# A four-layer transformer kernel on one core: turned tiles among the dense products, weight casts in ScalarE's gaps, and a score bank for attention's last group

## The chip, the cores and the metric

The kernel runs on one core of one Trainium2 chip. The metric is the device time of one execution in microseconds, lower is better. A core has TensorE (PE, which loads weights through PEld), VectorE (DVE), ScalarE (ACT), GpSimd (POOL) and SyncE (SP, which here issues the DMAs). TensorE writes into eight PSUM banks of 2 KB a partition; the other engines read the results from there.

## The reference

Four layers work on 1,024 tokens of 256 features. Each layer is `x = x + s * silu(f)`, where `s` is a token mixer and `f` a feed-forward part, both computed from the same layer-normalised `xn`. The change touches the way from the third layer to the fourth, and the fourth layer's attention.

```
xn = layernorm(x)                       # third layer
s = attention over 16 heads @ w_dense
f = 8 gated experts, weighted per token
x = x + s * silu(f)
xn = layernorm(x)                       # fourth layer
q, k, v = xn @ wq.T, xn @ wk.T, xn @ wv.T      # 8 heads, q and k in two halves each
y = softmax(rms(q1) rms(k1)) v - lambda * softmax(rms(q2) rms(k2)) v   # causal
s = y @ wo.T * 0.2
f = fwht(silu(xn @ W1.T) * (xn @ W3.T)) @ W2.T
out = x + s * silu(f)
```

## The kernel before

Every engine has its own instruction list, written out by hand; the engines meet only at semaphores (`wait_ge`). The tokens stand in 8 tiles of 128 (t = 0 to 7) and in 4 quarters of two tiles (i = 0 to 3). For precision each product of two float32 matrices is made of three products of rounded parts: `product` (L102 to L104) multiplies rounded by rounded, rounded by rest and rest by rounded. The rounded part of an operand comes from a cast, mostly on ScalarE, and its rest from a subtraction on VectorE or GpSimd.

From the third layer to the fourth the work goes like this.

- TensorE makes the last expert's down products (banks 4 to 7) and the dense products of attention (banks 0 to 3) in two halves, tiles 0 to 3 and then tiles 4 to 7.
- VectorE adds the expert's result into `g_tok` (`add_expert`, L1943); ScalarE puts it through Silu (`gate_silu`, L2322); VectorE multiplies by the dense product and adds to x (`residual`, L1456 and L1457), takes mean and variance (`statistics`, L1462 to L1468); GpSimd raises to the power of -1/2 (`rsqrt`, L657); VectorE normalises (`normalised`, L1473).
- TensorE transposes the normalised tiles (`turn_xn`, L888) into bank i for quarter i, ScalarE casts the quarter from there (`turned`, L2131) and VectorE takes its rest (`turned_rest`, L1480). Only then can TensorE make q, k and v of the tiles in that quarter (`qkv_rows`), which ScalarE evicts (`qkv_copy`, L2380 and L2383).
- TensorE's order is: all dense products, turned tiles 0 to 3, q/k/v of tiles 0 to 2, turned tiles 4 to 7, q/k/v of tiles 3 to 7. Its q/k/v products rotate over the bank pairs 6-7, 4-5 and 0-1.
- VectorE's order is: residuals and normalised tiles of the first half, `add_expert` of tiles 4 to 7, the rests of quarters 0 and 1, and then the same for the second half.
- ScalarE also casts the fourth layer's gate weights in four parts (L2474), and GpSimd subtracts to get their rests (L853), two parts at a time. These rests stand ahead of the gate and up products (`w_gate3`, `w_up3`), which follow the q/k/v products on TensorE. GpSimd takes the four `rsqrt(3)` before the gate rests, and the squares for the rms (L859) after them.

Attention of the fourth layer runs over 24 units (`UNITS3`): a unit is a pair of key tiles for a half of the queries of one group of four heads. `scores3` (L1373) writes a unit's scores for two heads at a time into one of three pairs of banks, 0-1, 2-3 and 4-5, in turn; ScalarE takes the exponential (L2511); for the units on the diagonal GpSimd multiplies by the causal mask, two instructions of two heads each (L875); `values3` (L1387), two units later, multiplies by v and by ones. The units of one (group, half) add up in one bank: the 16 results (`MIXES3`) alternate between banks 6 and 7, and VectorE divides (`normalise`, a reciprocal at L2079 and a product at L2081). So the last result, made of units 22 and 23, waits until the result two before it is divided. Behind the attention TensorE makes the down products, each waiting for a rest that VectorE takes (L2093), and the output products.

Of the kernel before, what the change touches and what calls it, by code (L numbers as in the profile page):

```python
# [45 lines left out]
E2 = 8  # L46
# [73 lines left out]
def build(nc, a, out, layers=4):  # L120
    ctx = ExitStack()
    with ctx:
# [210 lines left out]
        LAG3 = 2  # L333
        HID3_AT, HID3_BEHIND = (9, 12), (6, 8)
# [128 lines left out]

        SPLIT = [True, True, True, True]

        QKV_BANK = [None, None, (0, 6), (6, 4, 0)]
        QKV_TURNED = [None, None, (0, 0), (0, 0, 1)]
# [176 lines left out]
        def _(pool):  # L644
# [195 lines left out]
            if layers > 3:  # L840
# [30 lines left out]
                for u in DIAGONAL3:  # L871
                    for i in range(2):
# [7 lines left out]
        def _(pe):  # L880
# [301 lines left out]
            def qkv_rows(w, w_hi, layer, tiles=range(NT)):  # L1182

                turns = len(QKV_BANK[layer])
                for t in tiles:
                    if t >= turns:
                        pe.wait_ge(qkv_done, 2 * (NT * (layer - 2) + t - turns) + 2)
                    b0 = QKV_BANK[layer][t % turns]
                    turned(layer, QKV_TURNED[layer][t] if t < turns else t // 2)
# [74 lines left out]
            if layers > 2:  # L1264
# [44 lines left out]
                for b in range(B):  # L1309
# [5 lines left out]
                    for t in tiles:  # L1315
# [4 lines left out]
                        mm.then_inc(s_ready, 1)  # L1320
            if layers > 3:

                turn_xn(3, range(ST))
                pe.wait_ge(wq_split, 2)
                pe.wait_ge(e2_done, E20 + 8 * E2)
                qkv_rows(w_qkv3, w_qkv3_hi, 3, range(3))
                turn_xn(3, range(ST, NT))
                qkv_rows(w_qkv3, w_qkv3_hi, 3, range(3, NT))
# [50 lines left out]
                def mix3(m, u, which):  # L1379
# [3 lines left out]
                    for kt, at, q0, w in blocks_of(u):  # L1383
                        for hh in range(4):
                            head = 4 * c + hh
                            lhs = ones[:, 0:32] if which else v3[:, ST * b + kt, 32 * head:32 * head + 32]
                            mm = pe.matmul(bank[6 + m % 2][32 * hh:32 * hh + 32, 256 * which + q0 - 256 * h:256 * which + 256],  # L1387
# [5 lines left out]
                def values3(u):  # L1393
                    g, h, k = UNITS3[u]
                    m = MIXES3.index((g, h))
                    if u in DIAGONAL3:
                        pe.wait_ge(causal_done, 2 * DIAGONAL3.index(u) + 2)
                    else:
                        pe.wait_ge(exp3_done, 2 * u + 2)
                    if u == GROUPS3[m][0] and m >= 2:  # L1400
# [34 lines left out]
        def _(dve):  # L1435
# [469 lines left out]
            if layers > 2:  # L1905
# [101 lines left out]
                if layers > 3:  # L2007
                    add_expert(E2 - 1, 1, last=True, tiles=range(ST, NT))
                    rests(3, 0)
                    residuals(2, 1)  # L2010
                    rests(3, 1)
            if layers > 3:
# [59 lines left out]
                def normalise(m):  # L2072
                    g, h = MIXES3[m]
                    b, c, j = g // 4, g // 2 % 2, g % 2
                    o = bank[6 + m % 2]
# [18 lines left out]

                for m in range(len(MIXES3)):
                    normalise(m)
# [27 lines left out]
        def _(act):  # L2124
# [248 lines left out]
            def qkv_copy(layer, first=0, end=NT, between=None):  # L2373
                for t in range(first, end):
                    act.wait_ge(qkv_ready, NT * (layer - 2) + t + 1)
                    b0 = QKV_BANK[layer][t % len(QKV_BANK[layer])]
# [88 lines left out]
            if layers > 3:  # L2465

                turned(3, (0, 1))
                gate_silu(2, (2, 3))
                qkv_copy(3, 0, 2)
                turned(3, (2, 3))  # L2470
                qkv_copy(3, 2, 3)
                act.wait_ge(wgo3_in, 32)
# [122 lines left out]
```

## Time and profile before

| what | value |
|---|---|
| time, median of 3 runs | 840.95 us (840.45 to 841.15) |
| the profiled execution's own time | 839.71 us |
| its span in the trace | 837.9 us |
| TensorE busy | 826.0 us, 99% of the span |
| VectorE busy | 624.9 us, 75% |
| ScalarE busy | 478.4 us, 57% |
| GpSimd busy | 471.2 us, 56% |
| granted TensorE clock | 1.00 over the span |

The span runs from the first to the last instruction of the trace; the execution's own time has 1.81 us more around it. A busy share says how long an engine had an instruction in it. A matmul's end is modelled, and matmuls overlap, so the distance between the starts of two matmuls tells what one costs, and its own duration does not.

### The profile page before, as it was taken

The page shows a single profiled execution, that of the slowest core. Times are in us where ns is not written, and L with a number is a line of the kernel's source. Part 1 is how long each engine was busy: PE and PEld are TensorE (multiplying, and loading weights), DVE is VectorE, ACT ScalarE, POOL GpSimd, SP SyncE. Part 2 cuts the span into 40 slices and gives each one's busy share as a digit, 9 for nine tenths or more (in the row PEclk, how much of TensorE's full clock was granted, in tenths as well). Part 3 has the DMA queues.
Part 4 walks back from the last instruction along what each step waited for, and adds up shares of the span by engine and source line. Part 5 has one row for each costly group of instructions (what it writes and reads, how often), then busy time and mean ns, then how long its engine had stood idle before and what let it go on. Part 6 is the DMA issues. An engine that isn't in the chain of part 4 may idle for free.

```text
span 837.9 us, 15615 instructions
## 1 busy us (share of the span) xinstructions
PE 826.0 (99%) x5436; PEld 709.6 (85%) x5436; DVE 624.9 (75%) x1267; ACT 478.4 (57%) x953; POOL 471.2 (56%) x327
## 2 busy tenths in 40 slices
PE   8999999999999999999999999999999999999998
PEld 7888888888867899999999888888889988876688
DVE  6899999999997665665567788687676785436767
ACT  3666666666674565655553475743453435367743
POOL 6676767677684855575757021019948316718820
PEclk9999999999999999999999999999999999999999
DMA  8101010000005385556313150011111010030001
GB/s 340 43 20 38 19 38 19 28 28 19 19 1 188 146 283 184 184 166 193 110 32 94 59 201 14 1 52 51 38 38 38 14 63 1 1 151 4 2 2 51
DMA packets 23345, 62.19 MB, mean 74 GB/s; under 512 B 3137, under 2 KB 13633, under 8 KB 20225
## 3 DMA queue, kind: packets, MB, share of 16 engines
q1 hardware_dynamic: 21760, 57.35, 19.8%
q0 software_dynamic: 1536, 4.20, 1.6%
q8 instruction: 30, 0.49, 0.2%
q14 instruction: 19, 0.15, 0.1%
HBM read 50.00 MB, written 8.39 MB: 70 GB/s over the span
## 4 chain that ended last, share of the span: by engine, by line
PE 88%; DVE 6%; POOL 2%; ACT 2%; issue 1%; DMA 1%; SPq 0%; DVEq 0%; POOLq 0%
PE banks L102 26%; PE banks L104 26%; PE banks L103 26%; PE banks L1387 3%; POOL arenaC L875 1%; PE banks L1373 1%; PE banks L1023 1%; PE banks L967 1%; PE banks L966 1%; DVE x L1457 1%; DVE arenaB L1892 1%; PE banks L888 1%; PE banks L1010 1%; PE banks L1056 1%; DMA arenaC<-in_wqkv 1%
## 5 line engine op out<-in xcount | busy, mean ns | idle before, releaser
L2153 ACT ACTIVATE banks<-banks,small 128x512 f32<-128x512 f32 x128 | 84.9, 664 | 70.8 <-DVE small L1522 70.8
L1522 DVE TENSOR_REDUCE small<-banks 128x1 f32<-128x512 f32 x128 | 86.7, 677 | 4.4 <-PE banks L104 4.4
L104 PE MATMUL banks<-arenaC_rounded,arenaD_rounded 128*128 128x512 f32 (+1 forms) x256 | 89.4, 349 | 0.0
L102 PE MATMUL banks<-xnT_rounded,arenaD_rounded 128*128 128x512 f32 x224 | 87.8, 392 | 1.1 <-POOL arenaC_rounded L741 0.9
L103 PE MATMUL banks<-s_tok_rounded,arenaD_rounded 128*128 128x512 f32 x224 | 87.2, 389 | 0.0
L104 PE MATMUL banks<-xnT_rounded,arenaD_rounded 128*128 128x512 f32 x192 | 74.8, 390 | 0.0
L104 PE MATMUL banks<-xnT_rounded,arenaC_rounded 128*128 128x512 f32 x192 | 74.7, 389 | 0.0
L102 PE MATMUL banks<-arenaC_rounded 128*128 128x512 f32 (+1 forms) x192 | 70.9, 369 | 1.2 <-DVE arenaC L1537 0.6
L1537 DVE SCALAR_TENSOR_TENSOR arenaC<-banks,small,arenaC 128x512 f32<-128x512 f32 x96 | 71.2, 741 | 0.0
L103 PE MATMUL banks<-arenaD_rounded,arenaC_rounded 128*128 128x512 f32 (+1 forms) x192 | 67.9, 354 | 0.0
L727 POOL TENSOR_TENSOR arenaD_rounded<-arenaC,ones 128x512 fp32r<-128x512 f32 x30 | 31.3, 1042 | 47.4 <-DVE arenaC L1537 46.5
L102 PE MATMUL banks<-arenaB_rounded,arenaC_rounded 128*128 128x256 f32 (+2 forms) x172 | 55.4, 322 | 0.0
L104 PEld LDWEIGHTS banks<-arenaC_rounded,arenaD_rounded 128*128 128x128 f32 x256 | 48.0, 188 | 5.0
L657 POOL TENSOR_TENSOR rstd<-veps,mhalf 128x2 f32<-128x2 f32 x16 | 12.2, 762 | 69.1 <-DVE veps L1468 69.1
L788 POOL TENSOR_TENSOR arenaD_rounded<-arenaD,arenaB_rounded 128x1024 fp32r<-128x1024 f32 (+1 forms) x12 | 37.6, 3147 | 23.7 <-ACT arenaB_rounded L2217 23.7
L102 PEld LDWEIGHTS banks<-xnT_rounded,arenaD_rounded 128*128 128x128 f32 x224 | 42.0, 188 | 10.0 <-POOL arenaC_rounded L741 1.0
L102 PE MATMUL banks<-xnT_rounded,arenaB_rounded 128*128 128x512 f32 x128 | 50.3, 393 | 0.0
L103 PEld LDWEIGHTS banks<-s_tok_rounded,arenaD_rounded 128*128 128x128 f32 x224 | 42.1, 188 | 8.5
L103 PE MATMUL banks<-arenaC_rounded,arenaB_rounded 128*128 128x320 f32 (+2 forms) x144 | 49.1, 341 | 0.0
L722 POOL TENSOR_TENSOR arenaD_rounded<-arenaD,arenaC_rounded 128x512 fp32r<-128x512 f32 x32 | 41.5, 1297 | 12.6 <-ACT arenaD L2144 12.6
L104 PE MATMUL banks<-arenaB_rounded,arenaC_rounded 128*128 128x256 f32 (+1 forms) x140 | 46.1, 329 | 0.0
L103 PE MATMUL banks<-arenaB_rounded,arenaC_rounded 128*128 128x320 f32 (+2 forms) x140 | 45.8, 327 | 0.0
(445 smaller groups left out, 2689.3 us busy)
## 6 DMA issues: line engine op xcount, KB each, us to landing
arenaD<-in_wexp SPq DMA_DIRECT2D x8, 1060.0 KB, 5.8
arenaD<-in_wexp SPq DMA_DIRECT2D x8, 1024.0 KB
arenaC<-in_wqkv SPq DMA_DIRECT2D x16, 384.0 KB, 3.0
arenaD<-in_wexp SPq DMA_DIRECT2D x8, 512.0 KB, 3.6
slots<-arenaB SPq DMA_DIRECT2D x1, 2560.0 KB, 9.9
arenaB<-in_sw SPq DMA_DIRECT2D x1, 2084.0 KB, 7.5
arenaC<-in_wo SPq DMA_DIRECT2D x1, 2048.0 KB, 15.3
arenaC<-slots SPq DMA_DIRECT2D x8, 256.0 KB, 3.2
```

Of the source, the lines that this page charges most:

```text
L102: pe.matmul(o, r(lhs[0]), r(rhs[0]), start=start, stop=False)
L103: pe.matmul(o, r(lhs[0]), r(rhs[1]), start=False, stop=False)
L104: return pe.matmul(o, r(lhs[1]), r(rhs[0]), start=False, stop=stop)
L657: pool.tensor_tensor(rstd[:, sl], veps[:, sl], mhalf[:, sl], ALU.pow).then_inc(ln_rstd, 1)
L722: pool.tensor_tensor(r(klo[q][:, sl]), klo[q][:, sl], rounded(kT[q][:, sl]), ALU.subtract).then_inc(klo_done, 1)
L727: pool.tensor_tensor(r(acc_hi[b]), acc[b], ones[:, 0:1].to_broadcast([P, S]), ALU.mult).then_inc(acc_rounded, 1)
L788: pool.tensor_tensor(r(v), v, rounded(h), ALU.subtract).then_inc(w_split, 1)
L875: pool.tensor_tensor(d, d, con[:, C_CAUSAL:C_CAUSAL + P].unsqueeze(1).unsqueeze(1).to_broadcast([P, 2, 2, P]), ALU.mult).then_inc(causal_d ...
L1387: mm = pe.matmul(bank[6 + m % 2][32 * hh:32 * hh + 32, 256 * which + q0 - 256 * h:256 * which + 256], lhs, prob3[u % 4][:, hh, at:at + w], ...
L1522: dve.tensor_reduce(negmax[:, n % 4:n % 4 + 1], bank[3 + n % 4][:, :], AX.X, ALU.max, negate=True).then_inc(max_done, 1)
L1537: ins = dve.scalar_tensor_tensor(acc[n // ST], prob[n % 4], inv, acc[n // ST], ALU.mult, ALU.add)
L2153: act.activation(prob[r], prob[r], ACT.Exp, bias=negmax[:, r:r + 1], accum_out=rowsum[:, r:r + 1]).then_inc(exp_done, 1)
```

## The change

It has two parts. Between the layers, TensorE turns tiles 0 and 1 ahead of the last dense product, tiles 2 and 3 behind it, tiles 4 and 5 behind the q/k/v products of tile 2, and tiles 6 and 7 behind those of tile 4. The q/k/v products use an explicit list of banks (`QKV_BANK`) and of the tile whose eviction they wait for (`QKV_BEFORE`). VectorE takes the rest of quarter 0 right behind the first half's normalised tiles, and does the second half quarter by quarter. ScalarE mixes the weight casts, the Silu of the fourth quarter and the evictions in another order. In attention, the last result goes to bank 4 and its wait for an earlier division is left out, and the second two heads of unit 22 are masked by VectorE (`masked_last`, ahead of the division of result 13) in place of GpSimd.

```
@@ -331,6 +331,10 @@
         DIAGONAL3 = [n for n, (g, h, k) in enumerate(UNITS3) if k == 2 * h]
         GROUPS3 = [[u for u, v in enumerate(UNITS3) if v[0:2] == mix] for mix in MIXES3]
         LAG3 = 2
+
+        def mix_bank(m):
+            return 6 + m % 2 if m < len(MIXES3) - 1 else 4
+
         HID3_AT, HID3_BEHIND = (9, 12), (6, 8)
         TURNS3 = {6: (0, 1), 8: (2, 3), 10: (4, 5), 12: (6, 7)}
 
@@ -461,10 +465,12 @@
 
         EXP0, ACC0, VALS0, HID0, Y0, TURN0, ROWS0, GU0, E20 = 4, 4, 1, 0, 2, 2, 32, 2, 8
 
+        causal_dve = gold_done
         SPLIT = [True, True, True, True]
 
-        QKV_BANK = [None, None, (0, 6), (6, 4, 0)]
-        QKV_TURNED = [None, None, (0, 0), (0, 0, 1)]
+        QKV_BANK = [None, None, (0, 6) * 4, (4, 0, 4, 0, 6, 0, 4, 6)]
+        QKV_BEFORE = [None, None, (None, None, 0, 1, 2, 3, 4, 5), (None, None, 0, 1, None, 3, 2, 4)]
+        QKV_TURNED = [None, None, (0, 0), (0, 1)]
         HAD_BANK, LIN_BANK = (0, 1, 4, 5), (0, 1, 4, 5)
         TURNED_BANK = [(0, 1, 2, 3), (2, 3, 6, 7), (4, 5, 2, 3), (0, 1, 2, 3)]
         S0_BANK = (0, 5)
@@ -869,7 +875,7 @@
                 pool.tensor_tensor(r(v), v, rounded(hi), ALU.subtract).then_inc(had_done, 1)
 
                 for u in DIAGONAL3:
-                    for i in range(2):
+                    for i in range(2 if u != DIAGONAL3[-1] else 1):
                         pool.wait_ge(exp3_done, 2 * u + i + 1)
                         d = prob3[u % 4].rearrange("p h (k n) -> p h k n", k=2)[:, 2 * i:2 * i + 2, :, 0:P]
                         pool.tensor_tensor(d, d, con[:, C_CAUSAL:C_CAUSAL + P].unsqueeze(1).unsqueeze(1).to_broadcast([P, 2, 2, P]), ALU.mult
@@ -1181,12 +1187,11 @@
 
             def qkv_rows(w, w_hi, layer, tiles=range(NT)):
 
-                turns = len(QKV_BANK[layer])
                 for t in tiles:
-                    if t >= turns:
-                        pe.wait_ge(qkv_done, 2 * (NT * (layer - 2) + t - turns) + 2)
-                    b0 = QKV_BANK[layer][t % turns]
-                    turned(layer, QKV_TURNED[layer][t] if t < turns else t // 2)
+                    if QKV_BEFORE[layer][t] is not None:
+                        pe.wait_ge(qkv_done, 2 * (NT * (layer - 2) + QKV_BEFORE[layer][t]) + 2)
+                    b0 = QKV_BANK[layer][t]
+                    turned(layer, QKV_TURNED[layer][t] if t < 2 else t // 2)
                     n1 = D + E2 if layer == 2 else D
                     for o, w0, n in ((bank[b0][:, :], 0, 512), (bank[b0 + 1][:, 0:n1], 512, n1)):
                         for c in range(DC):
@@ -1318,14 +1323,20 @@
                                          [ctxT[:, c, t * P:(t + 1) * P], ctx_tok[:, t, c * P:(c + 1) * P]],
                                          [w_dense_hi[:, c, :], w_dense[:, c, :]], c == 0, c == DC - 1)
                         mm.then_inc(s_ready, 1)
+                        if layers > 3 and t == NT - 2:
+                            turn_xn(3, (0, 1))
             if layers > 3:
 
-                turn_xn(3, range(ST))
+                turn_xn(3, (2, 3))
                 pe.wait_ge(wq_split, 2)
+                pe.wait_ge(e2_done, E20 + 8 * (E2 - 1) + ST)
+                qkv_rows(w_qkv3, w_qkv3_hi, 3, range(3))
+                turn_xn(3, (4, 5))
+                qkv_rows(w_qkv3, w_qkv3_hi, 3, (3,))
                 pe.wait_ge(e2_done, E20 + 8 * E2)
-                qkv_rows(w_qkv3, w_qkv3_hi, 3, range(3))
-                turn_xn(3, range(ST, NT))
-                qkv_rows(w_qkv3, w_qkv3_hi, 3, range(3, NT))
+                qkv_rows(w_qkv3, w_qkv3_hi, 3, (4,))
+                turn_xn(3, (6, 7))
+                qkv_rows(w_qkv3, w_qkv3_hi, 3, (5, 6, 7))
                 pe.wait_ge(qkv_done, 4 * NT - 4)
 
                 def turn_qk(t):
@@ -1384,7 +1395,7 @@
                         for hh in range(4):
                             head = 4 * c + hh
                             lhs = ones[:, 0:32] if which else v3[:, ST * b + kt, 32 * head:32 * head + 32]
-                            mm = pe.matmul(bank[6 + m % 2][32 * hh:32 * hh + 32, 256 * which + q0 - 256 * h:256 * which + 256],
+                            mm = pe.matmul(bank[mix_bank(m)][32 * hh:32 * hh + 32, 256 * which + q0 - 256 * h:256 * which + 256],
                                            lhs, prob3[u % 4][:, hh, at:at + w],
                                            start=(u == GROUPS3[m][0] and at == 0 and which == 0), stop=(u == GROUPS3[m][-1] and at > 0 and which == 1),
                                            tile_position=(0, 32 * hh))
@@ -1393,11 +1404,14 @@
                 def values3(u):
                     g, h, k = UNITS3[u]
                     m = MIXES3.index((g, h))
-                    if u in DIAGONAL3:
+                    if u == DIAGONAL3[-1]:
+                        pe.wait_ge(causal_done, 2 * len(DIAGONAL3) - 1)
+                        pe.wait_ge(causal_dve, 2)
+                    elif u in DIAGONAL3:
                         pe.wait_ge(causal_done, 2 * DIAGONAL3.index(u) + 2)
                     else:
                         pe.wait_ge(exp3_done, 2 * u + 2)
-                    if u == GROUPS3[m][0] and m >= 2:
+                    if u == GROUPS3[m][0] and 2 <= m < len(MIXES3) - 1:
                         pe.wait_ge(norm3_done, m - 1)
                     mix3(m, u, 0)
                     mm = mix3(m, u, 1)
@@ -2005,10 +2019,18 @@
                 add_expert(E2 - 1, 1, last=True, tiles=range(ST))
                 residuals(2, 0)
                 if layers > 3:
-                    add_expert(E2 - 1, 1, last=True, tiles=range(ST, NT))
-                    rests(3, 0)
-                    residuals(2, 1)
-                    rests(3, 1)
+                    turned_rest(3, 0)
+                    add_expert(E2 - 1, 1, last=True, tiles=(4, 5))
+                    turned_rest(3, 1)
+                    residual(2, 2)
+                    statistics(3, 2)
+                    add_expert(E2 - 1, 1, last=True, tiles=(6, 7))
+                    normalised(3, 2)
+                    residual(2, 3)
+                    turned_rest(3, 2)
+                    statistics(3, 3)
+                    normalised(3, 3)
+                    turned_rest(3, 3)
             if layers > 3:
 
 
@@ -2072,7 +2094,7 @@
                 def normalise(m):
                     g, h = MIXES3[m]
                     b, c, j = g // 4, g // 2 % 2, g % 2
-                    o = bank[6 + m % 2]
+                    o = bank[mix_bank(m)]
                     dve.wait_ge(av_ready, m + 1)
                     if m:
                         dve.wait_ge(norm3_done, m)
@@ -2092,7 +2114,17 @@
                     v = hid3[:, :, t * P:(t + 1) * P]
                     dve.tensor_tensor(r(v), v, rounded(hid3_hi[t % 2]), ALU.subtract).then_inc(gu_split, 1)
 
+                def masked_last():
+
+                    u = DIAGONAL3[-1]
+                    dve.wait_ge(exp3_done, 2 * u + 2)
+                    d = prob3[u % 4].rearrange("p h (k n) -> p h k n", k=2)[:, 2:4, :, 0:P]
+                    dve.tensor_tensor(d, d, con[:, C_CAUSAL:C_CAUSAL + P].unsqueeze(1).unsqueeze(1).to_broadcast([P, 2, 2, P]), ALU.mult
+                                      ).then_inc(causal_dve, 1)
+
                 for m in range(len(MIXES3)):
+                    if m == len(MIXES3) - 3:
+                        masked_last()
                     normalise(m)
                     if m in HID3_BEHIND:
                         hid3_rest(HID3_BEHIND.index(m))
@@ -2373,7 +2405,7 @@
             def qkv_copy(layer, first=0, end=NT, between=None):
                 for t in range(first, end):
                     act.wait_ge(qkv_ready, NT * (layer - 2) + t + 1)
-                    b0 = QKV_BANK[layer][t % len(QKV_BANK[layer])]
+                    b0 = QKV_BANK[layer][t]
                     qk, v = (qkv2[:, t, 0:512], qkv2[:, t, 512:768]) if layer == 2 else (qk3[:, t, :], v3[:, t, :])
                     if layer == 2:
                         act.copy(z_raw[:, t, :], bank[b0 + 1][:, D:D + E2]).then_inc(z_copied, 1)
@@ -2465,16 +2497,23 @@
             if layers > 3:
 
                 turned(3, (0, 1))
-                gate_silu(2, (2, 3))
+                gate_silu(2, (2,))
                 qkv_copy(3, 0, 2)
-                turned(3, (2, 3))
+                gate_silu(2, (3,))
+                act.wait_ge(wgo3_in, 32)
+
+                def up_gate_round(parts):
+                    for n in parts:
+                        act.copy(r(part(arenaB, 1536 + 512 * n, 512)), part(arenaD, 3072 + 512 * n, 512)).then_inc(ff3_rounded, 1)
+
+                up_gate_round((0,))
+                turned(3, (2,))
                 qkv_copy(3, 2, 3)
-                act.wait_ge(wgo3_in, 32)
-                for n in range(4):
-                    act.copy(r(part(arenaB, 1536 + 512 * n, 512)), part(arenaD, 3072 + 512 * n, 512)).then_inc(ff3_rounded, 1)
-                    if n % 2:
-                        qkv_copy(3, 3 + n // 2, 4 + n // 2)
-                qkv_copy(3, 5)
+                up_gate_round((1,))
+                qkv_copy(3, 3, 4)
+                up_gate_round((2, 3))
+                turned(3, (3,))
+                qkv_copy(3, 4)
 
                 def queries3(t):
                     act.wait_ge(qkT_ready, t + 1)
```

## Rows read from the trace of the kernel before

**Rows 1.** The page, busy time of an engine, its share and its instructions.

```profile
PE 826.0 (99%) x5436; PEld 709.6 (85%) x5436; DVE 624.9 (75%) x1267; ACT 478.4 (57%) x953; POOL 471.2 (56%) x327
```

**Rows 2.** The timeline of TensorE between the layers: start, duration, instruction, count, idle before.

```profile
679.42 0.28 PE L102 MATMUL banks<-arenaB_rounded 128*128 128x256 f32 x1
...
680.12 1.04 PE L888 MATMUL banks<-con,xn 128*128 128x128 f32 x8
682.55 0.47 PE L102 MATMUL banks<-arenaB_rounded,xnT_rounded 128*128 128x512 f32 x1 [1.39 <-DVE arenaC_rounded L1480]
...
688.92 1.40 PE L888 MATMUL banks<-con,xn 128*128 128x128 f32 x8
690.07 0.48 PE L102 MATMUL banks<-arenaB_rounded,xnT_rounded 128*128 128x512 f32 x1
...
700.65 0.39 PE L102 MATMUL banks<-xnT_rounded,arenaB_rounded 128*128 128x512 f32 x1
```

**Rows 3.** The timeline of TensorE at sixteen earlier transposes.

```profile
666.97 1.91 PE L1306 MATMUL banks<-con,arenaB 128*128 128x128 f32 x16
668.63 0.36 PE L102 MATMUL banks<-xn_rounded,arenaD_rounded 128*128 128x256 f32 x1
```

**Rows 4.** The timeline of VectorE in the same stretch.

```profile
679.49 0.74 DVE L1473 TENSOR_SCALAR xn<-x,meanvar,rstd 128x256 f32<-128x256 f32 x2 [0.26 <-POOL rstd L657]
680.14 1.66 DVE L1943 SCALAR_TENSOR_TENSOR g_tok<-banks,small,g_tok 128x256 f32<-128x256 f32 x4
681.71 0.69 DVE L1480 TENSOR_TENSOR arenaC_rounded<-banks,xnT_rounded 128x512 fp32r<-128x512 f32 x1
...
685.50 0.69 DVE L1456 TENSOR_TENSOR g_tok<-g_tok,banks 128x512 f32<-128x512 f32 x1
...
688.02 0.17 DVE L1468 TENSOR_SCALAR veps<-meanvar 128x2 f32<-128x2 f32 x1
...
689.09 0.41 DVE L1473 TENSOR_SCALAR xn<-x,meanvar,rstd 128x256 f32<-128x256 f32 x1 [0.26 <-POOL rstd L657]
```

**Rows 5.** The timeline of ScalarE in the same stretch.

```profile
680.76 1.07 ACT L2131 CAST xnT_rounded<-banks 128x512 fp32r<-128x512 f32 x2 [7.42 <-PE banks L888]
681.72 1.16 ACT L2322 ACTIVATE g_tok<-g_tok 128x512 f32<-128x512 f32 x2
...
685.40 0.38 ACT L2383 COPY arenaC<-banks 128x256 f32<-128x256 f32 x1
```

**Rows 6.** The timeline of GpSimd in the same stretch.

```profile
692.82 4.78 POOL L853 TENSOR_TENSOR arenaD_rounded<-arenaD,arenaB_rounded 128x1024 fp32r<-128x1024 f32 x2 [3.76 <-ACT arenaB_rounded L2474]
```

**Rows 7.** The timeline of TensorE at attention's end.

```profile
800.57 0.83 PE L1387 MATMUL banks<-arenaC,ones 128*32 128x256 f32 x16
801.72 0.86 PE L1387 MATMUL banks<-arenaB,arenaC 128*32 128x256 f32 x16 [0.32 <-DVE arenaC L2081]
802.36 0.43 PE L1387 MATMUL banks<-arenaB,ones 128*32 128x256 f32 x4
```

**Rows 8.** The timelines of ScalarE and GpSimd at attention's end.

```profile
797.54 1.51 ACT L2511 ACTIVATE arenaB<-banks 128x768 f32<-128x768 f32 x2 [0.53 <-PE banks L1373]
...
798.87 2.54 POOL L875 TENSOR_TENSOR arenaB<-arenaB,con 128x512 f32<-128x512 f32 x2
```

**Rows 9.** The timeline of VectorE at attention's end and behind it.

```profile
799.36 1.76 DVE L2079 RECIPROCAL arenaC<-banks 128x256 f32<-128x256 f32 x1 [2.11 <-PE banks L1387]
...
809.14 1.23 DVE L2093 TENSOR_TENSOR arenaB_rounded<-arenaB,arenaD_rounded 128x1024 fp32r<-128x1024 f32 x1 [1.91 <-ACT arenaD_rounded L2500]
```

**Rows 10.** Lines L1918, L1473 and L2026 of VectorE, the second with shortest, median and longest ns.

```profile
663.37 1.80 DVE L1918 TENSOR_TENSOR arenaD_rounded<-arenaD,xn_rounded 128x512 fp32r<-128x512 f32 x1
...
L1473 DVE TENSOR_SCALAR xn<-x,meanvar,rstd x32: 404/408/420, 6.0 to 689.4; 128x256 f32<-128x256 f32 x32
...
710.03 0.29 DVE L2026 TENSOR_SCALAR small<-small 128x256 f32<-128x256 f32 x1
```

**Rows 11.** The timeline of GpSimd ahead of L1918's long case.

```profile
663.33 1.30 POOL L846 TENSOR_TENSOR arenaC_rounded<-arenaC,arenaB_rounded 128x512 fp32r<-128x512 f32 x1 [16.20 <-ACT arenaB_rounded L2457]
```

## The prediction

> **What bounds the kernel now.** I read the page first: TensorE is busy for 826.0 us of a span of 837.9 [rows 1], at the full granted clock all along. So only about 12 us can be won without taking matmuls away, and an edit that takes none away is worth exactly the TensorE waits that it ends. I then listed TensorE's gaps over the stretch that the change touches, from 667 us to the end, in its timeline.
>
> Between the layers there are two. The dense products end at 680.12, eight transposes follow, and the first q/k/v product starts at 682.55, released by VectorE's rest of quarter 0 [rows 2]. Sixteen transposes elsewhere take 668.63 - 666.97 = 1.66, so 0.104 each [rows 3]; eight need 0.83, and the first gap holds 2.43 - 0.83 = 1.60 of waiting. The second group of eight takes 690.07 - 688.92 = 1.15 [rows 2], so 0.32 is waiting: tiles 6 and 7 are normalised only from 689.09 on [rows 4]. Together 1.92.
>
> At attention's end the first products of unit 22 start at 801.72, behind a division on VectorE [rows 7]. The products before them started at 800.57. The same sixteen take 802.36 - 801.72 = 0.64 right after [rows 7], so unit 22 could have started at 800.57 + 0.65 = 801.22. That gap is worth 0.50; the trace calls 0.32 of it idle, since it counts from a modelled end.
>
> All that the change can give is therefore 1.92 + 0.50 = 2.42.
>
> **Between the layers, step by step.** No matmul, cast or subtraction is added or taken away; two groups of transposes become four, and SyncE's DMAs stay where they are. I follow the new order with the old durations.
>
> 1. Tiles 0 and 1 are turned at 679.42, where the last dense product started [rows 2]. They must be normalised by then: the pair 2 and 3 starts on VectorE at 679.49 [rows 4], so they are. Before, ScalarE's cast began 680.76 - 680.12 = 0.64 behind the first transpose [rows 2, 5], with four needed for it. Now it begins at 680.06 and, at half of 1.07 [rows 5], ends at 680.6.
> 2. VectorE is at its normalised tiles until 679.49 + 0.74 = 680.23 [rows 4], and then takes the rest at once, where before it first added the expert into four tiles (1.66) [rows 4]. The rest starts at about 680.68. Before, the first product stood 682.55 - 681.71 = 0.84 behind the rest's start [rows 2, 4]. So TensorE starts at 681.52, 1.03 earlier. Its own work by then ends at 679.42 + 8 x 0.104 + 0.70 (the dense tile) = 680.95: 0.57 of the wait stays, since the chain transpose, cast, rest is as long as it was.
> 3. Three tiles of q/k/v take 688.92 - 682.55 = 6.37, so 2.12 each [rows 2]. Tile 1 now needs quarter 1's rest, at 683.64. VectorE adds the expert into tiles 4 and 5 (0.83) and takes that rest until about 682.8. It is in time by 0.8.
> 4. Quarter 2: the residual starts at 682.8; residual and statistics take 688.02 - 685.50 = 2.52 up to the variance, and the normalised tiles start 689.09 - 688.02 = 1.07 later [rows 4], which is 686.4. They end at 687.15, and TensorE wants them at 681.52 + 6.37 = 687.89. In time. It turns them, makes tile 3 until 687.89 + 0.42 + 2.12 = 690.43, and needs quarter 2's rest there; the chain of step 2 gives it by 690.0.
> 5. Quarter 3 is the tight one. Its Silu stands on ScalarE behind the eviction of tile 1. Before, tile 0 left TensorE at 682.55 + 2.12 = 684.67 and its eviction ended at 685.40 + 0.38 = 685.78 [rows 2, 5], 1.1 later. Tile 1 now leaves at 685.76, so the Silu (0.58, half of 1.16 [rows 5]) ends at 687.45. The residual ends at 687.45 + 2 x 0.70 = 688.85, then quarter 2's rest comes in between until 689.8, statistics take 2.52 - 1.4 = 1.1, and the tiles start at 691.95. Tile 6 is normalised by 692.3 and tile 7 by 692.7. TensorE comes at 690.43 + 2.12 = 692.55 and turns tile 6 until 692.76. So it waits 0 to 0.2, where before it waited 0.32.
> 6. Tiles 5 to 7 follow: 692.55 + 0.42 + 6.37 = 699.34, to which I add 0.1 for step 5. Before, the gate products started at 700.65 [rows 2]. The gain is 1.2; two more changes between transposes and products, which no row prices apart, can take 0.1 to 0.2 of it.
>
> What must not become late is the gate rests on GpSimd, 4.78 for both [rows 6]. They need ScalarE's casts, of which the first pair is ready at about 690.7 (behind tile 2's eviction, 1.1 from 689.1 on, and 0.54 for a part of 512 columns, as half of 1.07 [rows 5]), and they stand behind the last `rsqrt`, which now ends at about 691.9 (before, it had ended ahead of 689.09). They run from 691.9 to 696.7 instead of 692.82 to 697.60, and the products want them at 699.4. They are covered by 2.7; without that cover each microsecond of lateness would cost one. The squares behind them gain only 0.9, where TensorE gains 1.2.
>
> **Attention's end.** The bank: without the division, unit 22 waits for its mask only. GpSimd's two masks run from 798.87 to 801.41 [rows 8], so the bank alone would give 801.72 - 801.45, about 0.3. The mask: GpSimd ends the first half at 798.87 + 1.27 = 800.14. VectorE can start the other at 797.54 + 1.51 = 799.05, when both exponentials are done [rows 8]; it is free, since its next division waits until 799.36 [rows 9]. The price on VectorE has no row of this kind. From below it is the 0.69 of a subtraction of the same 512 columns [rows 4]. From above it is 1.80: the row of L1918 with two SBUF inputs, started 0.04 behind a GpSimd instruction of 1.30 [rows 10, 11]. It looks like 1.26 of waiting and 0.6 of work. GpSimd's mask started first here too, so I take the end at 800.14 + 0.69 = 800.83. Even 799.05 + 1.80 = 800.85 is ahead of 801.22, so the whole 0.50 is won. Divisions 13 and 14 start up to 1.5 late; behind the last one VectorE had 1.91 idle ahead of L2093 [rows 9].
>
> The Trainium skill says the same of that pair (SBUF — State Buffer, section "SBUF: two separate sides"): GpSimd and a VectorE instruction with two SBUF inputs, or in a two-port mode, take one shared port pair as an exclusive lock for the whole instruction. By this rule, the trace agrees with L1918's 1.80 against 0.69.
>
> **The sum.** 1.2 + 0.5 = 1.7. The profiled execution would have a span of 836.2 and, with the same 1.81 around it, 838.0 instead of 839.71. The median of the runs is 1.24 above the profiled one, so the forecast is 840.95 - 1.7 = 839.25, which I round up to 839.3 for the two switches.
>
> **The rivals.** 0.2% of 840.95 is 1.68 us, about what a measurement of this kernel can tell from no change; the forecast stands at that bound.
>
> - Step 5 slips (17 in 100). Quarter 3's chain crosses three engines, with ScalarE's eviction in it; 0.5 to 1.0 more lateness at tile 6 goes straight to TensorE. Gain 0.7 to 1.2, time 839.7 to 840.2. For it: the margin is zero. Against: all durations are read from rows.
> - Only attention's end works, or the gain between the layers comes back as a wait among the gate products, because the squares and the root behind them gained less (8 in 100). Gain 0 to 0.6, time 840.4 to 841. Against it: the squares lose only 0.3 relative to TensorE.
> - More than forecast (7 in 100): the 0.57 of step 2 shrinks too, up to the full 2.42. Time 838.5.
> - Slower, by the port (8 in 100, half of it beyond 0.2%). GpSimd's first gate rest (2.39, half of 4.78 [rows 6]) now starts at 691.9, together with VectorE's last two normalised tiles; before, it started behind them. If L1473 has to wait as L1918 did, tile 6 comes at 691.9 + 2.39 + 0.35 = 694.6 and TensorE stalls by some 2.3: 841.6, no change to be told. If the second rest gets in ahead of tile 7 as well, it is 4.7: 840.95 - 1.7 + 4.7 = 843.95. It decides from a stall of 3.4 on. Against it: L1473 has one SBUF tensor as its input. The rival needs it to hold both ports all the same, and no row has it beside a long GpSimd instruction.
>
> A page speaks for this last rival. The Trainium skill (VectorE: DVE Perf Modes, section "The perf-mode tier table") lets a float32 `tensor_scalar` in SBUF run at twice the speed, with both read ports. By it L1473 would be locked out, and the result would be the 841.6 to 843.95 above. The trace speaks against it here: L1473, with its scalars read from SBUF, takes 408 ns for 256 columns, and L2026, with constants, 293 ns for the same 256 [rows 10]. Only L2026 looks like the faster mode.
>
> **How the numbers follow.** The forecast's case (60 in 100) spans 838.9 to 839.7, so gains of 1.25 to 2.05, with somewhat more of it below the bound of 839.27 than above in speed: 35 of the 60 are faster by over 0.2%. With the 7 for more, faster has 42 in 100; slower 5; no change to be told 53. The range of 838.5 to 841.0 takes in all but the slower rival and what lies outside of the sum.
>
> **What would show it.** The first q/k/v product starts 1.0 behind the last dense one (681.52 - 680.54, with 0.42 of transposes in it), not 2.43; VectorE's rest of quarter 0 directly behind its normalised tiles; no idle time at the second and fourth groups of transposes; GpSimd's gate rests about 0.9 earlier and the gate products 1.2 earlier; L1473 at 0.41 beside GpSimd; and unit 22 starting without a wait, with VectorE's mask ending ahead of it. The prediction is wrong if TensorE waits for tile 6, for a gate rest, or among the gate products, or if VectorE's mask takes over 2.1.

## The result, and the profile after

The changed kernel takes 845.67 us in the median (5 runs, 844.09 to 846.07), the kernel before beside it 841.04. The ratio is 1.0051, with a 95% interval of 1.004 to 1.0061: it is slower by 4.6 us, and the forecast was 1.7 us faster. The profiled execution took 845.67 with a span of 843.9, 6.0 above the span before.

I cut both spans at the same four events: the start of the last group that belongs to the dense products (the last dense tile before, tiles 0 and 1 turned after), the first gate product, the first score and the first down product.

| stretch | before | after | difference |
|---|---|---|---|
| up to the dense products' last tile | 679.42 | 680.85 | +1.43 |
| to the first gate product | 21.23 | 26.21 | +4.98 |
| to the first score | 47.26 | 47.35 | +0.09 |
| to the first down product | 56.97 | 56.43 | -0.54 |
| to the end | 33.02 | 33.06 | +0.04 |

The first 1.43 lies ahead of everything that the change touches. In the executions profiled below that point lies between 678.9 and 681.1, at both ends in kernels with the changed order, so it is no effect of the change. The stage with attention's end (the last but one) gave 0.54, where 0.5 was forecast. All of the loss is between the layers. These are TensorE's rows there, which answer to [rows 2]; the columns are start, duration, instruction, count and the idle time before it.

```profile
680.85 0.60 PE L894 MATMUL banks<-con,xn 128*128 128x128 f32 x4
...
682.95 0.47 PE L102 MATMUL banks<-arenaB_rounded,xnT_rounded 128*128 128x512 f32 x1 [0.35 <-DVE arenaC_rounded L1494]
...
689.29 0.60 PE L894 MATMUL banks<-con,xn 128*128 128x128 f32 x4
...
695.85 0.41 PE L894 MATMUL banks<-con,xn 128*128 128x128 f32 x2 [1.76 <-DVE xn L1487]
698.10 0.69 PE L894 MATMUL banks<-con,xn 128*128 128x128 f32 x2 [1.85 <-DVE xn L1487]
698.44 0.78 PE L102 MATMUL banks<-arenaB_rounded,xnT_rounded 128*128 128x512 f32 x1
...
707.06 0.39 PE L102 MATMUL banks<-xnT_rounded,arenaB_rounded 128*128 128x512 f32 x1
```

The first half went as planned: the first q/k/v product stands 2.10 behind the start of the last dense group, where it stood 3.13 before. Tiles 4 and 5 are turned without a wait. Then TensorE waits 1.76 for tile 6 and 1.85 for tile 7, and VectorE's line L1487 (L1473 before) is what it waits for. VectorE's and GpSimd's timelines, and the line's shortest, median and longest time, show why.

```profile
692.54 0.69 POOL L663 TENSOR_TENSOR rstd<-veps,mhalf 128x2 f32<-128x2 f32 x1 [4.80 <-DVE veps L1482]
693.19 4.71 POOL L859 TENSOR_TENSOR arenaD_rounded<-arenaD,arenaB_rounded 128x1024 fp32r<-128x1024 f32 x2
...
693.27 4.78 DVE L1487 TENSOR_SCALAR xn<-x,meanvar,rstd 128x256 f32<-128x256 f32 x2 [0.81 <-POOL rstd L663]
...
L1487 DVE TENSOR_SCALAR xn<-x,meanvar,rstd x32: 404/408/2434, 6.0 to 695.6; 128x256 f32<-128x256 f32 x32
```

GpSimd starts its first gate rest at 693.19, VectorE its tile 6 at 693.27. Two instructions that took 0.74 [rows 4] now take 4.78, next to the 4.71 of GpSimd's two, and end 0.15 behind them (698.05 and 697.90). A second loss is in the products behind. The windows give the busy time of each engine, then the granted clock of TensorE (PEclk).

```profile
core 0: us, PE busy (x) PEld busy (x) DVE busy (x) ACT busy (x) POOL busy (x), PEclk, DMA share, GB/s
692.50:698.44 5.94, 2.33 (x14) 1.76 (x13) 4.78 (x2) 1.42 (x4) 5.90 (x4) 0.84 0.00 0
698.44:703.30 4.86, 4.86 (x17) 4.09 (x16) 3.13 (x8) 1.98 (x5) 3.29 (x4) 0.50 0.02 3
703.30:708.00 4.70, 4.70 (x28) 4.08 (x27) 2.75 (x4) 1.84 (x5) 3.29 (x4) 0.99 0.00 0
```

Behind the two waits TensorE runs 4.86 us at 0.50, its lower level of 1.2 GHz, and loses half of that, 2.43 by this estimate. The clock fell here during the second wait: it was 1.00 up to 696 and 0.50 from 697 on. Attention's end, which answers to [rows 7 to 9], is clean: unit 22 follows unit 21 after 0.65 and without a wait, and VectorE's mask ends at 807.20.

```profile
805.37 1.29 POOL L881 TENSOR_TENSOR arenaB<-arenaB,con 128x512 f32<-128x512 f32 x1
...
805.57 1.63 DVE L2122 TENSOR_TENSOR arenaB<-arenaB,con 128x512 f32<-128x512 f32 x1 [1.83 <-ACT arenaB L2550]
...
807.05 0.83 PE L1398 MATMUL banks<-arenaC,ones 128*32 128x256 f32 x16
807.70 0.83 PE L1398 MATMUL banks<-arenaB,arenaC 128*32 128x256 f32 x16
```

### The profile page after: what moved, and what is told of

It reads as the page before. It is cut to its first block, busy times and chain, and to the rows that moved or that the text cites. A ratio compares the mean times of both kernels' runs of the same rounds, so it can differ in the third digit from the quotient of the medians.

```text
span 843.9 us, 15619 instructions
## 1 busy us (share of the span) xinstructions
PE 829.9 (98%) x5436; PEld 712.7 (84%) x5436; DVE 630.7 (75%) x1268; ACT 478.7 (57%) x953; POOL 470.0 (56%) x326
## 4 chain that ended last, share of the span: by engine, by line
PE 88%; DVE 6%; POOL 2%; ACT 2%; DMA 1%; issue 1%; SPq 0%; DVEq 0%; POOLq 0%
PE banks L102 26%; PE banks L103 26%; PE banks L104 26%; PE banks L1398 3%; POOL arenaC L881 1%; PE banks L1384 1%; PE banks L1029 1%; PE banks L973 1%; PE banks L972 1%; DVE xn L1487 1%; PE banks L894 1%; DVE arenaB L1906 1%; DMA arenaC<-in_wqkv 1%; PE banks L1016 1%; PE banks L1062 1%
```

## The experiments

The theory: GpSimd's two gate rests lock out VectorE's last two normalised tiles (3.6 us of waiting), and the half clock that follows costs up to 2.4 more. The main rival: the new order itself (quarter 3's residual behind an eviction, other banks) makes the tiles late.

**The two parts apart.** One kernel has the part between the layers alone, one attention's end alone, and one of attention's end only the bank. The edits are shortened; attention's end alone is the bank with `masked_last` and its waits added:

```
 # between the layers alone: from the changed kernel
-        def mix_bank(m): ...
-                    if m == len(MIXES3) - 3:
-                        masked_last()
 # bank only: from the kernel before
-                            mm = pe.matmul(bank[6 + m % 2][32 * hh: ...
+                            mm = pe.matmul(bank[mix_bank(m)][32 * hh: ...
-                    if u == GROUPS3[m][0] and m >= 2:
+                    if u == GROUPS3[m][0] and 2 <= m < len(MIXES3) - 1:
```

> The kernel before with the part between the layers alone; attention's end as before. Theory (the whole loss is made between the layers, and attention's end gives 0.5 us): 5.1 us slower than before, about 846.1, with both waits at tiles 6 and 7 and some 4.9 us at half clock. Rival (attention's end costs too, through VectorE's mask of 1.63 us): under 4.6 us slower.

> The kernel before with attention's end alone: last result in bank 4, VectorE masks one half. Theory: 0.5 us faster, about 840.5, with no wait of TensorE ahead of unit 22. Rival (the mask on VectorE delays the divisions so that something later waits): same or slower, 841.0 or more.

> The kernel before with the last result in bank 4 and its wait for a division left out; GpSimd still masks both halves. From the mask's end at 801.41 against the start at 801.72: 0.3 us faster, about 840.7, TensorE released by L875. If the mask on VectorE were of no use, this would equal the kernel with both edits (0.5 us faster).

Between the layers alone: 843.85 against 839.54 of the kernel before on that chip, ratio 1.005 (1.0036 to 1.0064), so 4.3 slower, with waits of 1.76 and 1.85 at tiles 6 and 7 again. That is less than the 5.1 expected, and below the 4.6 that I had set for the rival; but attention's end by itself costs nothing, as the next kernel shows. What was shorter is the stretch at half clock (the granted clock was 0.66 from 697 to 702), and it differs between executions. The fastest of the five took 842.48 with a granted clock of 1.00 over the span, two took 843.38 and 843.85 at 0.997, and the slowest two 844.24 and 844.87 at 0.995. So the half clock did not follow in every execution, and in the one without it the loss was 2.9. That the waits were the same in it is not shown: only the execution of 843.85 was traced. Attention's end alone: 839.06, 0.48 faster, but the interval of 0.9986 to 1.0004 does not exclude no change. The trace is sharper than the times: its sixteen products start 0.65 behind those of unit 21, at 801.25 instead of 801.72. With the bank alone, 839.65 against 839.68 in the times (0.9989 to 1.0007), and 0.91 between the two starts, so 0.24 of the 0.50 won, and TensorE is released by GpSimd's mask. The times of neither kernel tell it from no change; the two gains at attention's end are readings of traces.

**Taking the collision away.** GpSimd waits until all tiles are normalised; nothing else is altered.

```
                     if i == 0:
                         rsqrt(3)
+                        pool.wait_ge(xn_done, 4 * NT)
```

> The changed kernel, with one wait more: GpSimd takes the gate rests only when all tiles are normalised. Theory (GpSimd's two gate rests lock out VectorE's last two normalised tiles): L1487 falls from 2.43 us to 0.41 a tile, TensorE's waits of 1.76 and 1.85 us at the transposes of tiles 6 and 7 go to 0.2 or less, the granted clock stays at 1.00, and the time is the 1.7 us below the kernel before that the sum had without the collision: about 839.3. Rival (the loss comes from the new order of the chain itself, residual behind eviction, or from the new banks): the waits stay, time 844 to 846.

838.37 against 839.54, ratio 0.9987 (0.9978 to 0.9996): 1.17 faster than the kernel before. Its rows:

```profile
691.50 0.73 DVE L1488 TENSOR_SCALAR xn<-x,meanvar,rstd 128x256 f32<-128x256 f32 x2 [0.80 <-POOL rstd L663]
...
692.31 4.75 POOL L860 TENSOR_TENSOR arenaD_rounded<-arenaD,arenaB_rounded 128x1024 fp32r<-128x1024 f32 x2 [0.85 <-DVE xn L1488]
...
692.15 0.60 PE L895 MATMUL banks<-con,xn 128*128 128x128 f32 x4
...
694.02 0.73 DVE L2040 TENSOR_TENSOR lam_in<-lam_in 128x32 f32<-128x32 f32 x1
...
694.89 2.23 DVE L2040 TENSOR_TENSOR lam_in<-lam_in 128x32 f32<-128x32 f32 x1
...
710.50 0.50 PE L102 MATMUL banks<-xnT_rounded,arenaB_rounded 128*128 128x512 f32 x1 [0.16 <-ACT arenaC L2530]
```

The two tiles take 0.73 again, the four transposes at 692.15 have no wait, and the clock is 1.00 throughout. The new order of the chain and the new banks are kept, so the rival falls. But 1.17 is less than 1.7. From turned tiles 0 and 1 to the first gate product it takes 698.88 - 679.09 = 19.79, a gain of 1.44, more than the 1.2 forecast. From there to the first score it takes 48.08, where it took 47.26: 0.82 comes back as new waits among the gate and up products. By the distances between starts, 0.37 of it is at the fourth up product, behind VectorE's second multiplication, and 0.45 at the fifth gate product, behind the third Silu. The last row shows the second one, of which the trace calls 0.16 idle.

**Cutting the lock into pieces.** The changed kernel, with each gate rest as four instructions of 256 columns:

```
-                        v, h = part(arenaD, 3072 + 2048 * i + 1024 * n, 1024), part(arenaB, 1536 + 2048 * i + 1024 * n, 1024)
-                        pool.tensor_tensor(r(v), v, rounded(h), ALU.subtract).then_inc(ff3_split, 1)
+                        for w in range(PIECES if i == 0 else 1):
+                            size = 1024 // (PIECES if i == 0 else 1)
+                            v, h = (part(m, at + 2048 * i + 1024 * n + size * w, size) for m, at in ((arenaD, 3072), (arenaB, 1536)))
+                            ins = pool.tensor_tensor(r(v), v, rounded(h), ALU.subtract)
+                        ins.then_inc(ff3_split, 1)
```

> The changed kernel with each of GpSimd's two gate rests cut into four instructions of 256 columns, some 0.65 us each. Theory (the loser waits for the end of the one instruction that holds the port, not for a queue of them): each of the last two normalised tiles takes 0.7 to 1.1 us in place of 2.43, TensorE's waits there sum to about 1 us, the clock stays at 1.00, time about 840.5. Rival (VectorE waits until GpSimd has nothing more to do): tile 6 waits for all pieces, 4.8 us or more, time 845 or more.

```profile
691.53 5.70 POOL L862 TENSOR_TENSOR arenaD_rounded<-arenaD,arenaB_rounded 128x256 fp32r<-128x256 f32 x8
...
691.61 1.55 DVE L1491 TENSOR_SCALAR xn<-x,meanvar,rstd 128x256 f32<-128x256 f32 x2 [0.80 <-POOL rstd L664]
...
693.21 0.44 PE L898 MATMUL banks<-con,xn 128*128 128x128 f32 x2 [0.23 <-DVE xn L1491]
```

838.37 against 839.68, ratio 0.9985 (0.9976 to 0.9995). The two tiles take 1.55 instead of 4.78, and the trace shows one wait of TensorE there, of 0.23. The stall follows the length of the one instruction that stands in the way: VectorE gets in between two pieces. The time is 1.3 below the kernel before on that chip, where I had expected 0.45 (840.5 against 840.95). The tiles' remaining lateness did reach the first gate product (699.76 - 679.19 = 20.57, against 19.79 with the rests behind the tiles). From there to the first score it took 47.37, with 0.7 less of the waits among the gate products, so both orders come out alike.

**Which instructions are locked out.** In the kernel before VectorE is idle beside the gate rests. I gave it four instructions there, on 256 columns in SBUF each:

```
+                dve.wait_ge(ff3_rounded, 7)
+                probe = part(small, 820, 256)
+                link(dve.tensor_reduce(probe[:, 0:1], con[:, 0:256], AX.X, ALU.add))
+                link(dve.bn_stats(probe[:, 0:6], con[:, 0:256]))
+                link(dve.tensor_scalar(probe, con[:, 0:256], meanvar[:, 7, 0:1], rstd[:, 7:8], ALU.subtract, ALU.mult))
+                link(dve.tensor_scalar(probe, con[:, 0:256], -0.5, 1.5, ALU.mult, ALU.add))
```

> The kernel before; VectorE, idle there, waits for the same cast as GpSimd's first gate rest and then makes four more instructions of 256 columns in SBUF, each behind the one before, whose results nobody reads: a reduce, a bn_stats, a tensor_scalar with two scalars from SBUF (as L1473) and a tensor_scalar with two constants (as L2026). Theory (VectorE instructions that run in a two-port mode wait for GpSimd's instruction to end, and L1473 is one of them, though it takes 408 ns): reduce and bn_stats take their 0.4 us beside GpSimd; the first tensor_scalar ends with GpSimd's first rest (some 1.5 us or more), the second with its second rest (some 2.4 us). Rival A (every VectorE instruction on SBUF waits): reduce takes 2.4 and bn_stats 2.4. Rival B (scalars from SBUF are what must wait, not the mode): only the third is long and the fourth takes 0.29.

```profile
692.47 4.81 POOL L853 TENSOR_TENSOR arenaD_rounded<-arenaD,arenaB_rounded 128x1024 fp32r<-128x1024 f32 x2 [3.76 <-ACT arenaB_rounded L2480]
...
692.42 0.42 DVE L2021 TENSOR_REDUCE small<-con 128x1 f32<-128x256 f32 x1 [0.47 <-ACT arenaB_rounded L2480]
692.88 0.43 DVE L2022 BATCH_NORM_STATS2 small<-con 128x6 f32<-128x256 f32 x1
693.34 1.69 DVE L2023 TENSOR_SCALAR small<-con,meanvar,rstd 128x256 f32<-128x256 f32 x1
695.07 2.38 DVE L2024 TENSOR_SCALAR small<-con 128x256 f32<-128x256 f32 x1
```

This is one execution. The reduce and the statistics take 0.42 and 0.43 beside GpSimd (the reduce starts 0.05 ahead of GpSimd's rest, the statistics in the middle of it). The `tensor_scalar` with two scalars from SBUF ends at 695.03, within 0.2 of the end of GpSimd's first rest, and the one with constants at 697.45, within 0.2 of the end of the second (697.28). Both theories that I had set against mine fall: neither does every VectorE instruction wait, nor is it the scalars from SBUF. A third form shows by accident in the kernel whose gate rests wait for the normalised tiles. Two small `tensor_tensor` of 32 columns with both inputs in SBUF (L2040 in its rows above), which take 0.18 each in the kernel before, stand there beside the gate rests and take 0.73 and 2.23.

**What the clock costs.** The changed kernel again, and two kernels in which TensorE fills its two waits with products that nobody reads (`FILL` is 14 a tile in one and 7 in the other):

```
-                turn_xn(3, (6, 7))
+                pe.wait_ge(qkv_done, 2 * NT + 2 * 2 + 2)
+                for t in (6, 7):
+                    for n in range(FILL):
+                        pe.matmul(bank[5][:, 0:P], ones[:, :], ones[:, :], start=True, stop=True)
+                    turn_xn(3, (t,))
```

> The changed kernel; ahead of the transposes of tile 6 and of tile 7 TensorE makes 14 products of ones by ones each, about 1.5 us, into a bank that nobody reads. They fill its waits and end ahead of the tiles. Theory (of the 4.6 us lost, some 2.4 are the half clock of 4.86 us that follows the waits): the tiles still come late, the granted clock stays at 1.00, and the time is about 843.3. Rival (the clock falls whatever TensorE does there): half clock for some 4.9 us all the same, and 845.7 or more.

> The changed kernel again, unaltered, as the partner of the next two on the same chip. Theory: 4 to 5 us slower than the kernel before, both waits of 1.8 us at tiles 6 and 7, and a stretch at half clock behind them whose length differs between executions, so that the times spread by 1 to 2 us.

> As the filled kernel, with 7 products of ones by ones ahead of each of the two tiles in place of 14 (14 took 3.29 us and made tile 7 late by itself). Theory: the tiles still come 1.8 us late each, the granted clock stays at 1.00 throughout, and the time lies below the unfilled one by what the half clock costs there: 1 to 2.4 us, at about 3 us above the kernel before. Rival (the clock has no part in the loss): the same time as the unfilled one, within 0.4 us.

With 14 a tile the clock held (0.999 to 1.0 over the span), but the filling took 3.29 a tile instead of the 1.5 I had counted, and made tile 7 late by itself; 844.14 against 839.54 (843.3 expected, with the kernel before at 841.0) says nothing on the clock's price. With 7 a tile it is clean. On one chip, with the kernel before at 840.74, the changed kernel takes 844.14, ratio 1.0048 (1.0033 to 1.0062), and the filled one 842.80, ratio 1.0025 (1.0016 to 1.0034). TensorE's rows in the filled one (each filling product has two records, so x14 is seven), and then the window behind the waits, first of the changed kernel, then of the filled one:

```profile
693.41 1.72 PE L1342 MATMUL banks<-ones 128*128 128x128 f32 x14
695.35 0.41 PE L895 MATMUL banks<-con,xn 128*128 128x128 f32 x2 [0.21 <-DVE xn L1492]
695.60 1.73 PE L1342 MATMUL banks<-ones 128*128 128x128 f32 x14
697.71 0.41 PE L895 MATMUL banks<-con,xn 128*128 128x128 f32 x2 [0.38 <-DVE xn L1492]
```

```profile
697.49:701.10 3.61, 3.61 (x12) 3.02 (x13) 2.28 (x7) 1.35 (x3) 2.12 (x3) 0.53 0.00 0
```

```profile
697.50:701.10 3.60, 3.40 (x19) 2.99 (x20) 2.32 (x8) 2.19 (x5) 2.21 (x3) 1.00 0.02 5
```

The tiles are as late (the second by 0.1 more), the filled kernel still loses 2.1, and the clock does not fall. So the half clock cost 844.14 - 842.80 = 1.3 in this pair of medians; the slowest filled execution (843.39) is faster than the fastest unfilled one (843.65). From turned tiles 0 and 1 to the first gate product it is 25.40 against 23.92, 1.48. The same distance gives the price of the waits: 23.92 with the tiles late and the clock held, 19.79 with neither, so 4.13. That is more than the 3.6 of the idle times, which count from modelled ends. With these the profiled execution of the changed kernel adds up: 4.13 of waits and 26.21 - 23.92 = 2.29 of half clock, less the 1.44 and the 0.54 gained, plus the 0.09 of the table's third row, is 4.53, where the spans differ by 6.0 - 1.43 = 4.6 behind the point of the first cut.

**The rest of the gain.** On top of the kernel whose gate rests stand behind the normalised tiles, ScalarE takes the third gate product's Silu ahead of the root, and VectorE its Newton step one product later:

```
-                    if n == 1:
+                    if n == 2:
                         act.wait_ge(root_step, 1)
...
-                    if n == 1:
+                    if n == 2:
                         newton()
```

> The kernel with the gate rests behind the normalised tiles, and one more edit: ScalarE takes the Silu of the third gate product ahead of the square root for the rms, and VectorE its Newton step one product later. That kernel has 0.82 us of waiting in TensorE's gate products (48.08 from the first of them to the scores, against 47.26 in the kernel before), released by the third Silu, which stands behind the square root. Theory (that wait is the rest of the gain that the sum had): it goes, 0.8 us faster than with the gate rests behind alone, 2.0 us below the kernel before. Rival (the square root, 0.4 later, makes something else late): no gain, 1.2 below the kernel before.

839.45 against 840.74, ratio 0.9983 (0.9974 to 0.9992): 1.3 to 1.4 below the kernel before, not 2.0, and too near its partner's 1.17 to be told from it. From the first gate product to the first score it takes 748.59 - 700.91 = 47.68, against 48.08 in its partner and 47.26 before, so half of the 0.82 is gone. The wait behind the third Silu is gone, as expected. The other half is the wait of the fourth up product, 0.40 here, behind VectorE's second multiplication, which stands behind the reciprocal for the root (708.40, 1.75 long); I had counted it to the Silu too. By its ratio it is the fastest order that was run, within the intervals of the others.

## Why the prediction was wrong, point by point

- **What bounds the kernel** was right for the gain. For the loss, "exactly the TensorE waits" left something out: the waits also brought the clock down, and then the products themselves took longer.
- **Steps 1 to 4** held within 0.1. The gain at the first product is 3.13 - 2.10 = 1.03, as forecast.
- **Step 5 is the step that failed**, in the duration of its last two instructions. It was right as a chain: quarter 3's tiles start 693.27 - 680.85 = 12.4 behind the start of that stretch, against 12.5 forecast. But I kept 0.41 a tile [rows 4], and so a wait of 0 to 0.2, though the same working had moved GpSimd's gate rests onto the tiles. They took 2.4 each, and TensorE waited 1.76 and 1.85.
- **The rival "slower, by the port"** had this mechanism. I priced it at 4.7 of stall and gave it 8 in 100, and half of that to the case that came. I set it low because L1473 takes 408 ns and L2026 293 for the same columns [rows 10], and read that as L1473 not holding both ports. The probe and the removal of the collision show that the duration did not tell: both forms wait for the end of GpSimd's instruction. The Trainium skill's table (VectorE: DVE Perf Modes, section "The perf-mode tier table") gives `tensor_scalar` on float32 in SBUF twice the speed, by way of both read ports. On the ports the trace agrees: 2.43 instead of 0.41. On the speed it does not for the form with scalars from SBUF: 408 ns, where the form with constants takes 293. The Trainium skill's rule of an exclusive lock for the whole instruction (SBUF — State Buffer, section "SBUF: two separate sides") was right as well, and the trace agrees: the stall ends 0.15 behind GpSimd's instruction, and with pieces it shrinks from 4.78 for the two tiles to 1.55.
- **The price of the stall** had two terms. The waits gave 1.76 + 1.85 = 3.6 of idle time, and 4.1 by the starts of the products, against the rival's 4.7. The second I had not in the sum at all: the half clock behind them, 1.3 to 1.5 in the pair that isolates it, and 2.3 in the profiled execution. It is why the result lies 1.7 above the rival's 843.95 and not below it.
- **"The gain comes back among the gate products"** (8 in 100) was waiting behind it. I had counted that the squares lose 0.3 to TensorE; they lost 1.2. In the kernel without the collision they start at 697.02, 1.86 ahead of the first gate product, where they had 3.1 before (697.60 to 700.65), partly through the 0.85 that GpSimd waits there. It cost 0.82 of the 1.44 gained.
- **Attention's end** was right: 0.5 in the trace (0.48 in the times, which do not exclude no change), VectorE's mask takes 1.63 and ends 0.54 behind GpSimd's half (807.20 and 806.66), and the bank alone gives half of it.

The sum of the parts, with the collision away, is 1.44 - 0.82 + 0.54 = 1.16, and 1.17 was measured. Without the collision the change is faster than before, but below my 1.7.

## What to carry to other kernels

When an edit moves an instruction of GpSimd in time, look at what VectorE does beside its new place as well as at its own queue. A `tensor_scalar` on float32 in SBUF, or a `tensor_tensor` with two SBUF inputs, waited here until GpSimd's instruction ended (2.43 and 2.23 at the longest). Letting GpSimd wait for VectorE removed the stall, and cutting GpSimd's instruction into pieces left 0.8 of it for two tiles; both kernels were faster than the one before. A short stall of TensorE is to be priced with the clock behind it.

## What was not expected of the hardware

- An instruction's own duration did not show whether it waits for GpSimd: 408 ns for 256 columns with scalars from SBUF, 293 with constants, and both end with GpSimd's instruction (1.69 and 2.38 us), where a reduce and a bn_stats take 0.42 and 0.43.
- Around two waits of 1.8 us, with two transposes between them, TensorE went from 2.4 to 1.2 GHz. In one trace that came during the second wait, and 4.9 us of products ran at the lower level; in two others it came with the first products behind the waits, and 3.6 us of them did. With the same waits filled with products (0.21 and 0.38 left), it stayed at 2.4. How long the lower level lasts differs between executions of one kernel: the changed kernel's took 846.07 at a granted clock of 0.996 over the span and 844.09 at 0.998, and of the kernel with the part between the layers alone, one execution kept 1.00 and took 842.48, the slowest 844.87 at 0.995. Why it differs was not tried.
